# Flash-style attention on one core: exact exponentials of VectorE's low parts in PSUM, side jobs moved, maxima and their rows re-timed

## The chip, the cores and the metric

One core of a Trainium2 chip runs the whole program. The metric is the device time of one execution in microseconds. The kernel before takes 243.28 us, the median of 3 runs (242.67 to 243.59). Engines are named TensorE (PE), VectorE (DVE), ScalarE (ACT), GpSimd (POOL) and SyncE (SP, which issues the DMAs).

## The reference

For each of 8 images `x` of 128 channels and 32 x 32 = 1024 pixels:

```
q = Wq x + bq        (64 x 1024)
k = Wk x + bk        (64 x 1024)
v = Wv x + bv        (128 x 1024)
attn = softmax(q^T k, over the keys)
out  = gamma * (v attn^T) + x
```

All in float32. The kernel keeps the precision by splitting operands into a part rounded to fp32r (hi) and a remainder (lo).

## The kernel before, in words

**Tiling.** An image is 16 steps, 8 images make 128 steps. A step `s` is two key tiles (256 keys) against 256 queries. Four steps (`PART_STEPS`) make a part `u`: the same 256 queries against all 1024 keys; `j` is the place in the part, `k` the place in the image, and a half image (512 queries) is a chunk `c`.

**Stages of a step.** In `score_tile` TensorE computes the scores, transposed, into one of two banks of `scores`: four matmuls of 256 columns (L592 and L593), where the second of each pair adds the low part of q and, in one extra row, minus the maximum. ScalarE's `exponentials` reads them twice: it writes the exact exponential `weight` (L778) and the rounded one `weight_hi` (L781), in a ring of 8 steps. A subtraction makes `weight_lo` in bf16, on GpSimd (L472) or, for the steps that `low_on_dve` names, on VectorE (L878). `sums_hi` adds up `weight_hi` times the values (four matmuls of 258 columns, L612), and after the fourth step of a part `sums_lo` adds the low parts (16 matmuls of 130 columns, L626). A part uses two of the four banks of `sums`, and parts take turns. ScalarE copies the columns of the low values out (L787), VectorE inverts, adds (L889, L883) and writes the outputs (`finish`, L903), two steps after the low sums.

**Order of the work.** Every engine has its own queue, written out by hand as a loop over steps. TensorE's loop step `s` issues the scores of step `s + 2` (`AHEAD`), then the maxima of `max_jobs(s)`, then the sums of step `s - 2` (`LAG`), the low sums where `(s - 2) % 4 == 3`, then `side_jobs(s)`. So a step with low sums is one with `s % 4 == 1`. ScalarE's loop step does the exponentials of `s + 2`, the copy of low sums, and its half of the side jobs; VectorE's does its half of the side jobs of `s - 1`, the maxima of `s`, its subtraction for `s + 1`, and the ends of parts; GpSimd's the subtraction for `s + 1` and then one of its own jobs (low part of x, the bias on x turned, values in bf16).

**Maxima.** The exact maximum over the keys of each query is needed before the scores of its chunk: a matmul of 512 columns into a bank of `work` (L548) and a maximum by VectorE (L847), 8 for a chunk, one for each query tile and half of the keys. They run about a chunk and a half ahead, mostly one to a step; `EARLY_MAXES` is the table for steps 0 to 17. For image 0 TensorE turns the column of maxima into a row ("mt" jobs, L553), which ScalarE writes into `q_lomax`; later ones go by DMA (`send_max_row`).

**The two work banks.** Maxima and side jobs share two banks, taken in the strict turn of `WORK_ORDER`. Each job waits in `take_bank` until the job two places before it has been read out: for a maximum by VectorE's maximum, for "qk" (projection of q and k, L535 to L537) by VectorE's `qk_lo` (L838), which itself follows ScalarE's rounding (L743), for "v" (L542) by VectorE's `v_lo` (L843), which follows L754.

**DMAs.** SP issues everything from one queue in program order: `spread(n)` copies the rounded q and k of image n to their places on other partitions after the last qk job of n and after all scores of image n-2; its first four DMAs (L341 to L345) release the first maxima of image n, the other two its scores.

## Time and profile before

| what | value |
|---|---|
| median of 3 runs | 243.28 us (242.67 to 243.59) |
| the profiled execution: its time | 242.75 us |
| its span on the core | 241.0 us |
| TensorE busy, matmuls | 224.3 us, 93% |
| VectorE busy | 182.1 us, 76% |
| ScalarE busy | 176.9 us, 73% |
| GpSimd busy | 190.3 us, 79% |
| L878, VectorE's low parts | 30 times, 47.7 us, mean 1590 ns |
| L472, GpSimd's low parts | 98 times, 133.9 us, mean 1388 ns |
| chain that ended last | TensorE 74%, VectorE 15%, no visible wait 5%, ScalarE 3% |

How to read it: the span is what the profiler saw on the core, the execution's own time is 1.75 us longer. Matmul rows show how long one takes from start to end; in a dense stretch the next one starts long before, so the distance between starts tells the throughput. A row of the timeline gives the start in us, the duration, engine, line, operation, output and inputs, and in brackets the idle time before it and what ended it. The scores group that begins TensorE's loop step `s` marks the beginning of that step: step 6 begins at 27.50, step 16 at 54.58, step 32 at 82.85, step 38 at 91.88, step 45 at 103.83, step 46 at 107.71, step 48 at 110.18 and step 57 at 123.52.

### The profile page before, as it was taken

To read this page: it belongs to the slowest core of one execution; us is meant where nothing else is said; L and a number is where in the kernel's file an instruction comes from. 1 tells how busy PE (TensorE), PEld (TensorE's weight loads), DVE (VectorE), ACT (ScalarE), POOL (GpSimd) and SP (SyncE) were. 2 spreads that over 40 slices of the span, in tenths; PEclk is the share of its full clock that TensorE was granted. 3 is DMA by queue.
4 is the path that set the end of the run, shared out by engine and by line. 5 is a ranking of instruction groups with operands and counts; after the bars stand their busy time and mean duration, and the time that the engine had idled before them with its cause. 6 is when DMAs were issued, how large, how long until landed. Compare 5 with 4: busy or idle time off the path is not lost.

```text
span 241.0 us, 5343 instructions
## 1 busy us (share of the span) xinstructions
PE 224.3 (93%) x1864; PEld 207.2 (86%) x1864; DVE 182.1 (76%) x341; ACT 176.9 (73%) x342; POOL 190.3 (79%) x165
## 2 busy tenths in 40 slices
PE   6798946999998999989998999989999999999994
PEld 5466936888998999989998999989998999999994
DVE  1678396778888698779888698778898697689224
ACT  2488950675878688768888688768888688778980
POOL 8759991576898689879898689878898677897782
PEclk9999995899999999999999999999999999999999
DMA  3657600058510946048520847039400853010111
GB/s 104 186 222 169 182 0 0 4 119 191 167 51 3 222 85 218 2 99 209 125 98 0 209 98 220 2 86 221 127 10 0 192 116 131 4 44 3 44 48 44
DMA packets 17882, 24.43 MB, mean 101 GB/s; under 512 B 9920, under 2 KB 10688, under 8 KB 17856
## 3 DMA queue, kind: packets, MB, share of 16 engines
q1 hardware_dynamic: 17552, 23.96, 38.3%
q8 instruction: 15, 0.25, 0.4%
q10 hardware_dynamic: 304, 0.13, 0.2%
q14 instruction: 11, 0.09, 0.1%
HBM read 8.59 MB, written 4.19 MB: 53 GB/s over the span
## 4 chain that ended last, share of the span: by engine, by line
PE 74%; DVE 15%; issue 5%; ACT 3%; DMA 1%; ACTq 0%
PE sums L612 21%; PE sums L626 13%; PE work L548 10%; PE scores L592 10%; PE scores L593 9%; DVE neg_max L847 8%; PE work L542 6%; DVE weight_lo L878 4%; ACT values L754 2%; DVE y_sb L903 1%; DMA w_qk<-in_L_conv_Wk 1%; PE sums L548 1%; PE scores L644 1%; PE work L644 1%; PE work L536 0%
## 5 line engine op out<-in xcount | busy, mean ns | idle before, releaser
L472 POOL TENSOR_TENSOR weight_lo<-weight,weight_hi 128x512 bf16<-128x512 f32 x98 | 133.9, 1388 | 14.7 <-ACT weight_hi L781 14.7
L778 ACT ACTIVATE weight<-scores 128x512 f32<-128x512 f32 x128 | 76.9, 601 | 8.4 <-PE scores L593 2.0
L847 DVE TENSOR_REDUCE neg_max<-work 128x1 f32<-128x512 f32 x120 | 80.3, 682 | 3.3 <-PE work L548 3.3
L612 PEld LDWEIGHTS sums<-values,weight_hi 128*128 128x128 f32 x504 | 77.1, 190 | 4.7
L612 PE MATMUL sums<-values,weight_hi 128*128 128x258 f32 x504 | 81.0, 283 | 0.0
L781 ACT ACTIVATE weight_hi<-scores 128x512 fp32r<-128x512 f32 x128 | 77.0, 601 | 0.0
L592 PE MATMUL scores<-q_hihi,k_hilo 128*128 128x256 f32 x256 | 69.6, 294 | 0.0
L593 PE MATMUL scores<-q_lomax,k_hione 128*128 128x256 f32 x256 | 66.2, 281 | 0.0
L548 PE MATMUL work<-k_hilo,q_hihi 128*128 128x512 f32 x120 | 49.4, 416 | 9.9 <-DVE neg_max L847 9.2
L592 PEld LDWEIGHTS scores<-q_hihi,k_hilo 128*128 128x128 f32 x256 | 48.3, 189 | 1.3 <-issue 0.8
L593 PEld LDWEIGHTS scores<-q_lomax,k_hione 128*128 128x128 f32 x256 | 48.5, 189 | 0.8 <-issue 0.2
L878 DVE TENSOR_TENSOR weight_lo<-weight,weight_hi 128x512 bf16<-128x512 f32 x30 | 47.7, 1590 | 0.0
L626 PE MATMUL sums<-values_b,weight_lo 128*128 128x130 bf16 x496 | 35.2, 224 | 0.0
L548 PEld LDWEIGHTS work<-k_hilo,q_hihi 128*128 128x128 f32 x120 | 22.6, 189 | 13.9 <-DVE neg_max L847 7.6
L787 ACT ACTIVATE low_sum<-sums 128x256 f32<-128x256 f32 x31 | 11.9, 385 | 29.3 <-PE sums L626 29.3
L626 PEld LDWEIGHTS sums<-values_b,weight_lo 128*128 128x128 bf16 x496 | 29.7, 99 | 1.5
L889 DVE RECIPROCAL one_over<-sums 128x2 f32<-128x2 f32 x31 | 5.3, 171 | 31.5 <-ACT low_sum L787 31.2
L464 POOL TENSOR_SCALAR values_b<-values 128x512 bf16<-128x512 f32 x16 | 9.9, 620 | 20.4 <-ACT values L754 20.4
L453 POOL TENSOR_TENSOR x_lo<-x_sb,x_hi 128x512 fp32r<-128x512 f32 x12 | 15.5, 1292 | 7.1 <-ACT x_hi L750 7.1
L480 POOL TENSOR_TENSOR x_turned_sb<-x_turned_sb,gamma_bv 128x512 f32<-128x512 f32 x16 | 20.6, 1289 | 0.0
L903 DVE SCALAR_TENSOR_TENSOR y_sb<-sums,one_over,x_turned_sb 128x128 f32<-128x128 f32 x62 | 18.7, 343 | 0.7 <-DVE sums L883 0.4
L843 DVE TENSOR_TENSOR values<-work,values 128x512 fp32r<-128x512 f32 x14 | 9.7, 692 | 10.2 <-ACT values L754 10.2
(82 smaller groups left out, 165.2 us busy)
## 6 DMA issues: line engine op xcount, KB each, us to landing
x_turned_sb<-in_x_turned SPq DMA_DIRECT2D x8, 512.0 KB, 5.5
out<-y_sb SPq DMA_DIRECT2D x15, 256.0 KB, 2.8
x_sb<-in_x SPq DMA_DIRECT2D x7, 512.0 KB, 4.7
q_hihi<-qk_hi SPq DMA_DIRECT2D x12, 256.0 KB, 4.3
q_lomax<-qk_lo SPq DMA_DIRECT2D x7, 256.0 KB, 5.6
k_hione<-qk_hi SPq DMA_DIRECT2D x7, 256.0 KB, 5.4
k_hilo<-qk_hi SPq DMA_DIRECT2D x6, 256.0 KB, 3.2
k_hilo<-qk_lo SPq DMA_DIRECT2D x6, 256.0 KB, 6.2
```

The source lines that it names most:

```text
L472: pool.tensor_tensor(weight_lo[:, r], weight[:, r], weight_hi[:, r], ALU.subtract).then_inc(weight_lo_pool_done, 1)
L480: pool.tensor_tensor(place, place, bias, ALU.add).then_inc(with_bias_done, 1)
L548: pe.matmul(place, q_hihi[p][:, tile(t)], k_hilo[p][:, chunk(h)], start=True, stop=True).then_inc(mx_done, 1)
L592: pe.matmul(place, k_hilo[p][:, keys], q_hihi[p][:, queries], start=True, stop=False)
L593: last = pe.matmul(place, k_hione[p][:, keys], q_lomax[p][:, queries], start=False, stop=True)
L612: last = pe.matmul(sums[:, u % 2 * PAIR + it, 0:VCOLS], weight_hi[:, r, part_tile(kt, it)], values[p][:, key_tile(s, kt)], start=(j == 0 a ...
L626: last = pe.matmul(sums[:, u % 2 * PAIR + it, CHANNELS:VCOLS], weight_lo[:, i % RING, part_tile(kt, it)], values_b[p][:, key_tile(i, kt)], ...
L778: act.activation(weight[:, r], scores[:, s % 2], ACT.Exp)
L781: act.activation(weight_hi[:, r], scores[:, s % 2], ACT.Exp).then_inc(weight_hi_done, 1)
L847: dve.reduce_max(neg_max[:, t, h:h + 1], place, AX.X, negate=True).then_inc(neg_max_done, 1)
L878: dve.tensor_tensor(weight_lo[:, r], weight[:, r], weight_hi[:, r], ALU.subtract).then_inc(weight_lo_done, 1)
L903: dve.scalar_tensor_tensor(y_sb[:, h, at], sums[:, u % 2 * PAIR + it, CHANNELS:2 * CHANNELS], one_over[:, u % 2, it:it + 1], x_turned_sb[: ...
```

## The change

Four things are changed together.

1. `low_on_dve` names every third step of a part (`s % 4 == 2`), from the first part on: 32 steps for 30. For these steps ScalarE writes the exact exponential into the second bank of `sums` that the part is going to use (`exact_weights`), and VectorE subtracts from there. ScalarE waits first until the outputs of the part that used the bank before are written; TensorE waits for the subtraction before the first sums of the part.
2. The side jobs move: qk from steps 8 and 12 of an image to 6 and 10, v from 9 and 13 to 11 and 15. The jobs of ScalarE and GpSimd that feed them or follow them move too.
3. A chunk's maxima alternate between the two halves of the keys (`max_place`), image 0's second chunk is done one a step, the doubled ones lie at steps 7, 8, 11, 12 and 15, and its rows are turned two tiles at a time (`MAX_TURNS`).
4. At the start, image 1's projections of q and k move from ahead of the loop into steps 1 and 2, the second half of image 0's low q is made by one instruction of VectorE out of PSUM, and ScalarE takes the first exponentials ahead of the second q.

```diff
--- before.py
+++ after.py
@@ -37,8 +37,7 @@
 FIRST = ["k0", "q0", "k1", "q1"]
 
 
-DVE_LOW = (0, 4, 8, 12)
-ALL_ON_POOL = 8
+DVE_LOW = 2
 
 
 SPREAD_MX, SPREAD_REST = 4, 2
@@ -46,15 +45,17 @@
 
 
 EARLY = 18
-EARLY_MAXES = {0: (1, 1, 2), 1: (1, 3, 2), 2: (1, 5, 2), 3: (1, 7, 1),
-               6: (2, 0, 1), 7: (2, 1, 2), 8: (2, 3, 1), 9: (2, 4, 1), 10: (2, 5, 1), 11: (2, 6, 2),
-               12: (3, 0, 1), 13: (3, 1, 1), 14: (3, 2, 1), 15: (3, 3, 2), 16: (3, 5, 1), 17: (3, 6, 2)}
+EARLY_MAXES = {0: (1, 1, 1), 1: (1, 2, 1), 2: (1, 3, 1), 3: (1, 4, 1), 4: (1, 5, 1), 5: (1, 6, 1), 6: (1, 7, 1),
+               7: (2, 0, 2), 8: (2, 2, 2), 9: (2, 4, 1), 10: (2, 5, 1), 11: (2, 6, 2),
+               12: (3, 0, 2), 13: (3, 2, 1), 14: (3, 3, 1), 15: (3, 4, 2), 16: (3, 6, 1), 17: (3, 7, 1)}
+
+MAX_TURNS = {0: ("mt", 0, 1), 3: ("mt", 1, 0), 7: ("mt", 1, 1)}
 
 
 def max_jobs(s):
 
     if s < EARLY:
-        c, first, count = EARLY_MAXES.get(s, (0, 0, 0))
+        c, first, count = EARLY_MAXES[s]
         return [(c, i) for i in range(first, first + count)]
     chunk = (s + 14) // TILES
     return [(chunk, (s + 14) % TILES)] if chunk < CHUNKS else []
@@ -64,14 +65,12 @@
 
     b, k = divmod(s, STEPS)
     jobs = []
-    if b == 0 and k == 0:
-        jobs.append(("mt", 0, 1))
-    if b == 0 and k == 4:
-        jobs.append(("mt", 1, 0))
-    if k in (8, 12) and b + 2 < BATCHES:
-        jobs.append(("qk", b + 2, (8, 12).index(k)))
-    if k in (9, 13) and b + 1 < BATCHES:
-        jobs.append(("v", b + 1, (9, 13).index(k)))
+    if s in MAX_TURNS:
+        jobs.append(MAX_TURNS[s])
+    if k in (6, 10) and b + 2 < BATCHES:
+        jobs.append(("qk", b + 2, (6, 10).index(k)))
+    if k in (11, 15) and b + 1 < BATCHES:
+        jobs.append(("v", b + 1, (11, 15).index(k)))
     return jobs
 
 
@@ -91,7 +90,7 @@
 
 
 def low_on_dve(s):
-    return s >= ALL_ON_POOL and s % STEPS in DVE_LOW
+    return s % PART_STEPS == DVE_LOW
 
 
 def low_count(s):
@@ -117,7 +116,11 @@
 
 def max_place(i):
 
-    return i % CHUNK_TILES, i // CHUNK_TILES
+    return i // HALVES, i % HALVES
+
+
+def turn_count(c, half):
+    return HALVES * c + half + 1
 
 
 def half_count(n, h):
...
@@ -277,6 +281,10 @@
 
         def part_banks(u):
             return slice(u % 2 * PAIR, (u % 2 + 1) * PAIR)
+
+        def exact_weights(s):
+
+            return sums[:, s // PART_STEPS % 2 * PAIR + 1]
 
         def key_tile(s, kt):
             return s % PART_STEPS * PAIR + kt
...
@@ -433,13 +441,9 @@
                 pool.wait_ge(pool_setup, made + 4)
                 pool.memset(k_hione[p][HEAD:HEAD + 1, :].bitcast(fp32), 1.0).then_inc(pool_setup, 1)
                 made += 5
-            def first_q_lo(h):
-                pool.wait_ge(first_hi_done, FIRST.index(f"q{h}") + 1)
-                pool.wait_ge(first_q_done, h + 1)
-                pool.tensor_tensor(q_lomax[0][0:HEAD, chunk(h)], q_first[:, h], q_hihi[0][0:HEAD, chunk(h)],
-                                   ALU.subtract).then_inc(first_q_lo_done, 1)
-
-            first_q_lo(0)
+            pool.wait_ge(first_q_done, 1)
+            pool.tensor_tensor(q_lomax[0][0:HEAD, chunk(0)], q_first[:, :], q_hihi[0][0:HEAD, chunk(0)],
+                               ALU.subtract).then_inc(first_q_lo_done, 1)
             pool.wait_ge(pool_setup, made)
             pool.wait_ge(rest_loaded, 3 * 16)
             pool.tensor_scalar(gamma_bv[:, :], b_v[:, :], gamma_col[:, :], 1.0, ALU.mult, ALU.mult).then_inc(pool_setup, 1)
@@ -493,16 +497,14 @@
                     low_weights(s + 1)
                 if s == 0:
                     short_values(0, 1)
-                if s == 1:
-                    first_q_lo(1)
-                if s in (4, 6):
-                    add_bias((4, 6).index(s))
-                if k in (11, 15) and b + 1 < BATCHES:
-                    add_bias(2 * (b + 1) + (11, 15).index(k))
-                if k in (3, 7) and b + 2 < BATCHES:
-                    rest_of_x(b + 2, (3, 7).index(k))
-                if k in (10, 14) and b + 1 < BATCHES:
-                    short_values(b + 1, (10, 14).index(k))
+                if k in (0, 12) and s > 0 and b + k // 12 < BATCHES:
+                    short_values(b + k // 12, 1 - k // 12)
+                if s in (4, 8):
+                    add_bias((4, 8).index(s))
+                if b == 0 and k in (5, 9) or b > 0 and k in (1, 5) and b + 2 < BATCHES:
+                    rest_of_x(b + 2, (5, 9).index(k) if b == 0 else (1, 5).index(k))
+                if b == 0 and k in (10, 13) or b > 0 and k in (9, 13) and b + 1 < BATCHES:
+                    add_bias(2 * (b + 1) + k // 13)
 
         @block.tensor
         def _(pe):
...
@@ -606,6 +608,7 @@
                 if j == 0:
 
                     wait(pe, y_done, PAIR * (u - 1))
+                    pe.wait_ge(weight_lo_done, low_count(s + DVE_LOW))
                 pe.wait_ge(weight_hi_done, s + 1)
                 for kt in range(PAIR):
                     for it in range(PAIR):
@@ -684,9 +687,6 @@
             pe.wait_ge(first_hi_done, len(FIRST))
             for name, c, i in FIRST_MAXES:
                 do_max(c, i)
-            for h in range(HALVES):
-                pe.wait_ge(neg_max_done, CHUNK_TILES + PAIR + h + 1)
-                project_qk(1, h, sums[:, PAIR + h])
 
             for s in range(ALL_STEPS + LAG):
                 if s + AHEAD < ALL_STEPS:
@@ -705,6 +705,9 @@
                     sums_hi(s - LAG)
                     if (s - LAG) % PART_STEPS == PART_STEPS - 1:
                         sums_lo(s - LAG)
+                if s in (1, 2):
+                    pe.wait_ge(neg_max_done, CHUNK_TILES + PAIR + s)
+                    project_qk(1, s - 1, sums[:, PAIR + s - 1])
                 if s < ALL_STEPS:
                     for job in side_jobs(s):
                         do_job(job)
@@ -765,17 +768,21 @@
                 elif name == "v":
                     round_v(n, i, bank(bank_of(job)))
                 elif name == "mt":
-                    if n == 0:
-                        write_max_rows(2, 0, PART, CHUNK, bank(bank_of(job)))
-                    else:
-                        write_max_rows(3, CHUNK, 0, CHUNK, bank(bank_of(job)))
+                    write_max_rows(turn_count(n, i), n * CHUNK, i * PART, (i + 1) * PART, bank(bank_of(job)))
 
             def exponentials(s):
                 r = s % RING
                 act.wait_ge(scores_done, s + 1)
                 if s >= RING:
                     wait_low(act, s - RING)
-                act.activation(weight[:, r], scores[:, s % 2], ACT.Exp)
+                if low_on_dve(s):
+                    u = s // PART_STEPS
+                    wait(act, y_done, PAIR * (u - 1))
+                    if u == 0:
+                        act.wait_ge(neg_max_done, CHUNK_TILES + PAIR)
+                    if u == 1:
+                        act.wait_ge(qk_lo_done, HALVES)
+                act.activation(exact_weights(s) if low_on_dve(s) else weight[:, r], scores[:, s % 2], ACT.Exp)
 
                 wait(act, hi_step, s - RING + 1)
                 act.activation(weight_hi[:, r], scores[:, s % 2], ACT.Exp).then_inc(weight_hi_done, 1)
@@ -795,13 +802,10 @@
                 act.wait_ge(first_done, FIRST.index(f"q{h}") + 1)
                 act.activation(q_hihi[0][:, chunk(h)], place, ACT.Identity, bias=b_qq[:, :]).then_inc(first_hi_done, 1)
 
-            def first_whole_q(h, place):
-                act.activation(q_first[:, h], place[0:HEAD, :], ACT.Identity, bias=b_qq[0:HEAD, :]).then_inc(first_q_done, 1)
-
             first_k(0)
             first_q(0, bank(1))
-            first_whole_q(0, bank(1))
             first_k(1)
+            act.activation(q_first[:, :], bank(1)[0:HEAD, :], ACT.Identity, bias=b_qq[0:HEAD, :]).then_inc(first_q_done, 1)
             act.wait_ge(w_turned, 2)
             act.activation(w_v_t[:, :], bank(0)[:, 0:128], ACT.Copy, scale=gamma_col[:, :]).then_inc(w_v_ready, 1)
             round_v(0, 0, scores[:, 0])
@@ -809,25 +813,23 @@
 
             act.wait_ge(pool_setup, SETUP_MADE)
             write_max_rows(1, 0, 0, PART, scores[:, 1])
+            exponentials(0)
             first_q(1, bank(0))
-            exponentials(0)
             round_v(0, 1, sums[:, 0])
             exponentials(1)
-            round_qk(1, 0, sums[:, PAIR])
-            first_whole_q(1, bank(0))
 
             for s in range(ALL_STEPS):
                 b, k = divmod(s, STEPS)
                 if s + AHEAD < ALL_STEPS:
                     exponentials(s + AHEAD)
-                if s == 0:
-                    round_qk(1, 1, sums[:, PAIR + 1])
+                if s in (1, 2):
+                    round_qk(1, s - 1, sums[:, PAIR + s - 1])
                 if s >= LAG and (s - LAG) % PART_STEPS == PART_STEPS - 1:
                     take_low_sum((s - LAG) // PART_STEPS)
                 for job in side_jobs(s):
                     do_job(job)
-                if k in (2, 6) and b + 2 < BATCHES:
-                    round_x(b + 2, (2, 6).index(k))
+                if b == 0 and k in (4, 8) or b > 0 and k in (0, 4) and b + 2 < BATCHES:
+                    round_x(b + 2, (4, 8).index(k) if b == 0 else (0, 4).index(k))
 
             store_last(act, 1)
 
@@ -846,12 +848,17 @@
             def maximum(t, h, place):
                 dve.reduce_max(neg_max[:, t, h:h + 1], place, AX.X, negate=True).then_inc(neg_max_done, 1)
 
+            def round_second(half):
+                cols = slice(CHUNK_TILES + half * PAIR, CHUNK_TILES + (half + 1) * PAIR)
+                dve.wait_ge(neg_max_done, MAXES + CHUNK_TILES * (half + 1))
+                dve.tensor_reduce(neg_max_r[:, cols], neg_max[:, cols], AX.X, ALU.min).then_inc(neg_max_r_done, 1)
+
             def round_max(c):
                 cols = quarter(c % HALVES)
                 dve.wait_ge(neg_max_done, MAXES * (c + 1))
 
                 if c < 2 * HALVES:
-                    wait(dve, mt_done, c if c >= HALVES else 0)
+                    dve.wait_ge(mt_done, HALVES * (c - 1))
                 else:
                     wait_max_row(dve, c - HALVES)
                 dve.tensor_reduce(neg_max_r[:, cols], neg_max[:, cols], AX.X, ALU.min).then_inc(neg_max_r_done, 1)
@@ -861,7 +868,9 @@
                 dve.wait_ge(mx_done, max_count(c, i))
                 tile_of, keys = max_place(i)
                 maximum(h * CHUNK_TILES + tile_of, keys, bank(bank_of(("mx", c, i))))
-                if i == MAXES - 1:
+                if c == 1 and i % CHUNK_TILES == CHUNK_TILES - 1:
+                    round_second(i // CHUNK_TILES)
+                if c > 1 and i == MAXES - 1:
                     round_max(c)
 
             def do_job(job):
@@ -875,7 +884,7 @@
                 r = s % RING
                 dve.wait_ge(weight_hi_done, s + 1)
                 wait_lo_summed(dve, s - RING)
-                dve.tensor_tensor(weight_lo[:, r], weight[:, r], weight_hi[:, r], ALU.subtract).then_inc(weight_lo_done, 1)
+                dve.tensor_tensor(weight_lo[:, r], exact_weights(s), weight_hi[:, r], ALU.subtract).then_inc(weight_lo_done, 1)
 
             def add_low(u):
                 dve.wait_ge(low_sum_done, u + 1)
@@ -940,12 +949,14 @@
             for n in range(CHUNK_TILES, MAXES):
                 first_maximum(n)
             first_round_max(1)
-            for name, c, i in FIRST_MAXES:
-                do_max(c, i)
+            dve.wait_ge(first_hi_done, len(FIRST))
+            dve.scalar_tensor_tensor(q_lomax[0][0:HEAD, chunk(1)], bank(0)[0:HEAD, :], b_qq[0:HEAD, :],
+                                     q_hihi[0][0:HEAD, chunk(1)], ALU.add, ALU.subtract).then_inc(first_q_rest_done, 1)
             dve.wait_ge(v_hi_done, HALVES)
             dve.tensor_tensor(values[0][:, quarter(1), 0:CHANNELS], by_tiles(sums[:, 0]),
                               values[0][:, quarter(1), CHANNELS:2 * CHANNELS], ALU.subtract).then_inc(first_v_rest_done, 1)
-            rest_of_qk(1, 0, sums[:, PAIR])
+            for name, c, i in FIRST_MAXES:
+                do_max(c, i)
 
             for s in range(ALL_STEPS):
                 b, k = divmod(s, STEPS)
@@ -954,8 +965,8 @@
                         do_job(job)
                 for c, i in max_jobs(s):
                     do_max(c, i)
-                if s == 0:
-                    rest_of_qk(1, 1, sums[:, PAIR + 1])
+                if s in (1, 2):
+                    rest_of_qk(1, s - 1, sums[:, PAIR + s - 1])
                 if s + 1 < ALL_STEPS and low_on_dve(s + 1):
                     low_weights(s + 1)
                 if s >= LAG and (s - LAG) % PART_STEPS == PART_STEPS - 1:
```

## Rows read from the trace of the kernel before

**Rows 1.** The page, part 1: engine, busy us, share of the span, instructions.

```profile
PE 224.3 (93%) x1864; PEld 207.2 (86%) x1864; DVE 182.1 (76%) x341; ACT 176.9 (73%) x342; POOL 190.3 (79%) x165
```

**Rows 2.** List of waits: us in total, times, longest.

```profile
PE work L548 <- DVE neg_max L847: 9.2, 7, 5.6
```

**Rows 3.** Timeline of VectorE, steps 8, 43 and 115: start, duration.

```profile
30.91 6.64 DVE L878 TENSOR_TENSOR weight_lo<-weight,weight_hi 128x512 bf16<-128x512 f32 x1
...
102.70 1.72 DVE L878 TENSOR_TENSOR weight_lo<-weight,weight_hi 128x512 bf16<-128x512 f32 x1
...
222.00 0.69 DVE L878 TENSOR_TENSOR weight_lo<-weight,weight_hi 128x512 bf16<-128x512 f32 x1
```

**Rows 4.** Windows: length, busy of PE, PEld, DVE, ACT, POOL, granted clock, DMA.

```profile
32.00:36.00 4.00, 0.73 (x6) 0.48 (x4) 4.00 (x1) 1.66 (x3) 4.00 (x5) 1.00 0.00 0
36.00:40.00 4.00, 1.70 (x8) 1.54 (x9) 3.92 (x6) 0.00 (x0) 1.00 (x1) 0.58 0.00 0
```

**Rows 5.** Timeline of TensorE in image 0.

```profile
22.73 0.65 PE L612 MATMUL sums<-values,weight_hi 128*128 128x258 f32 x4
...
27.50 0.37 PE L592 MATMUL scores<-q_hihi,k_hilo 128*128 128x256 f32 x1
...
38.30 0.77 PE L548 MATMUL work<-k_hilo,q_hihi 128*128 128x512 f32 x1 [5.57 <-DVE neg_max L847]
...
43.15 0.50 PE L592 MATMUL scores<-q_hihi,k_hilo 128*128 128x256 f32 x1
```

**Rows 6.** Timeline of TensorE in the images behind it.

```profile
54.58 0.28 PE L592 MATMUL scores<-q_hihi,k_hilo 128*128 128x256 f32 x1
...
82.85 0.28 PE L592 MATMUL scores<-q_hihi,k_hilo 128*128 128x256 f32 x1
...
91.88 0.37 PE L592 MATMUL scores<-q_hihi,k_hilo 128*128 128x256 f32 x1
...
98.60 1.11 PE L542 MATMUL work<-w_v_t,x_sb 128*128 128x128 f32 x8
...
103.83 0.28 PE L592 MATMUL scores<-q_hihi,k_hilo 128*128 128x256 f32 x1
...
105.08 0.50 PE L548 MATMUL work<-k_hilo,q_hihi 128*128 128x512 f32 x1 [0.62 <-DVE neg_max L847]
...
107.71 0.36 PE L592 MATMUL scores<-q_hihi,k_hilo 128*128 128x256 f32 x1
...
110.18 0.28 PE L592 MATMUL scores<-q_hihi,k_hilo 128*128 128x256 f32 x1
...
110.66 0.39 PE L548 MATMUL work<-k_hilo,q_hihi 128*128 128x512 f32 x1
...
114.03 0.39 PE L548 MATMUL work<-k_hilo,q_hihi 128*128 128x512 f32 x1
...
123.52 0.28 PE L592 MATMUL scores<-q_hihi,k_hilo 128*128 128x256 f32 x1
...
124.14 0.50 PE L548 MATMUL work<-k_hilo,q_hihi 128*128 128x512 f32 x1
```

**Rows 7.** Durations: VectorE's L843 alone (min/median/max), two groups of ScalarE.

```profile
L843 DVE TENSOR_TENSOR values<-work,values x14: 691/692/694, 44.2 to 215.3; 128x512 fp32r<-128x512 f32 x14
...
L778 ACT ACTIVATE weight<-scores 128x512 f32<-128x512 f32 x128 | 76.9, 601 | 8.4 <-PE scores L593 2.0
...
L750 ACT ACTIVATE x_hi<-x_sb 128x512 fp32r<-128x512 f32 x12 | 7.6, 633 | 0.0
```

**Rows 8.** Timeline of VectorE: the low parts of v and of qk.

```profile
100.38 0.69 DVE L843 TENSOR_TENSOR values<-work,values 128x512 fp32r<-128x512 f32 x1 [0.67 <-ACT values L754]
...
124.44 0.75 DVE L838 SCALAR_TENSOR_TENSOR qk_lo<-work,b_qk,qk_hi 128x512 fp32r<-128x512 f32 x1 [0.36 <-ACT qk_hi L743]
```

**Rows 9.** The spread's fourth DMA: one issue, and the landing of all six.

```profile
106.60 1.14 SPq L345 DMA_DIRECT2D k_hilo<-qk_lo  x1
...
DMA to landing us min/median/max: 5.0/6.2/6.8
```

21 lines of the change are left out of this document (11 added, 10 removed).

## The prediction

> **What bounds the kernel now.** I read the page first: TensorE is busy for 224.3 of 241.0 us [rows 1], so only some 17 us, lead-in and tail included, can come from its pauses. In the list of waits the one large entry of TensorE is the matmul of the maxima (L548) waiting for VectorE to read a work bank: 9.2 us in 7 waits, 5.6 of them in one [rows 2]. VectorE's rows explain that one: the subtraction of the low parts in step 8 (L878), two SBUF inputs, lasts 6.64 us at 30.91 where the same instruction takes 0.69 in image 7 and 1.72 in a middle image [rows 3]. In the windows of those microseconds GpSimd is busy for all of 32 to 36 and for the first microsecond behind it, then idle; VectorE is busy with that one instruction, TensorE for 0.73 of 4 us [rows 4]. VectorE got its turn only when GpSimd ran dry. TensorE stood for 5.57 us and came back slow: from the max matmul of step 9 to the next step it took 4.85 us (38.30 to 43.15) [rows 5], against 2.63 for the same work in step 45 (105.08 to 107.71) [rows 6], and the granted clock of 36 to 40 was 0.58 [rows 4], mostly the 1.2 GHz level of the two. So image 0 lost about 5.6 + 2.2 us at one place.
>
> In a middle image TensorE is dense. An image takes 27.33 us (82.85 to 110.18). The max matmul follows the start of its step by 0.48 (110.18 to 110.66), but by 1.25 in step 45 (103.83 to 105.08) and by 0.62 in step 57 (123.52 to 124.14) [rows 6]. So 0.77 + 0.14 = 0.9 us an image is waiting behind the slow subtraction and the side job, and the rest is work. In image 7 nothing of this is left.
>
> **The change, part by part.**
>
> *Exact exponentials in PSUM.* ScalarE writes one 128x512 tile in four to a bank of sums, VectorE subtracts from there. The nearest row is L843, a subtraction with one PSUM and one SBUF input: 691 to 694 ns in all 14, whatever GpSimd did [rows 7]. From below the uncontested 0.69 with two SBUF inputs [rows 3] bounds it, from above the 1.72; I take 0.69. That is 32 x 0.69 = 22 us of VectorE for 30 subtractions of which the middle images' took 1.5 to 1.7. It is not TensorE's time by itself; what counts is that no subtraction stands in front of a maximum for over 0.69 us. GpSimd has 96 of them for 98, and nobody to wait for at the port. ScalarE's write to PSUM: no row has one of its own. It reads PSUM and writes SBUF in 601 ns and goes from SBUF to SBUF in 633 [rows 7], so I take 601, with 30 ns less or more: 1 us in all on an engine idle for a quarter of the span, at no cost to the end.
>
> A rule speaks against this edit. The Trainium skill (VectorE: DVE Perf Modes, section on the TRN2 errata) gives a vector instruction with a PSUM source 120 fixed cycles against 58 for SBUF, an estimated 65 ns more, 2 us of VectorE in all. The rows of 0.692 and 0.69 [rows 3, 7] show no such difference, and the sum is the same by either, since that engine would hide it. On the port, the same notes (SBUF — State Buffer, on the two sides of SBUF) say that GpSimd and a two-SBUF-input vector instruction exclude each other for one whole instruction; the 6.64 us show that the loser can lose several rounds, which is the case that costs here.
>
> *New waits.* ScalarE's exponential of step 4u+2 waits for the outputs of part u-2, and everything behind it in its queue with it. Their last instruction lands about 2.35 us after the start of step 4u-2 on TensorE (low sum, two small ops, one maximum, two output ops), the scores it needs land at 3.05: margin 0.7. TensorE's first sums of part u wait for that subtraction. It ends about 3.5 us after the start of step 4u and is wanted at 4.1: margin 0.6. I cost both at nothing in the steady part; what hides them is that TensorE's own step with low sums is long.
>
> *Side jobs.* qk goes to 6 and 10, v to 11 and 15. The second v now takes the bank of the qk job one step before. In the trace qk's low part is written at 125.19 (124.44 + 0.75), 1.67 us after the step that follows qk began (123.52) [rows 6, 8]. A plain step is 1.19, so v waits 0.5 in step 11. After v, its low part lands 2.47 us after v began (98.60 to 101.07) [rows 6, 8], just in time for the second max behind it. So a middle image loses 0.9 us of waits and gains 0.5: **0.4 us, four images, 1.6 us**. Image 1 also has a doubled max in its second step now, which becomes single: it took 28.27 us (54.58 to 82.85) against 27.33, so 0.9 more, **1.4 us** with its 0.4 rounded up. Image 6 has only v jobs and no such wait, image 7 none: nothing, though GpSimd's last three subtractions become two, up to 0.2 at the end.
>
> *Start.* Image 1's qk projections leave the place ahead of step 0, and image 0's second q loses one ScalarE and one GpSimd op for one op of VectorE. Followed by the durations above: scores 3 land at 19.0 and their exponentials end at 20.1, the rounding of qk (0.69) at 20.7, its low part (0.75) at 21.5, and only then comes the subtraction of step 2, 22.15. The first sums start there (before: 22.73 [rows 5]), after 1.6 us of idle. Behind them stand the second projection (0.66), two maxima turns and one read-out wait (0.3): step 6 starts at 28.5, 1.0 us later than before (27.50 [rows 5]). From step 6 to 16 the same jobs took 18.3 us in image 2 (91.88 to 110.18 [rows 6]), 17.4 without waits. To that come five second maxima at 0.24 (1.2), a turned row (0.15), and second maxima waiting for the low parts of qk in steps 7 and 11 (1.67 - 0.71, 1.0 each) and of v in step 12 (0.85). Step 16 starts at 50.1 instead of 54.58 [rows 6]: **4.5 us**.
>
> *DMAs.* No transfer is added, but SP's spread of the next image waits for step 13's scores, and the maxima of k=2 for its fourth DMA. Before, that DMA was issued 2.8 us after step 45 began (106.60) and landed 5.0 to 6.8 later [rows 9], with the max due 10.2 after that beginning (114.03 [rows 6]). Now due at 9.4, issued some 0.2 earlier, so landing at 7.6 to 9.4: just hidden, at no cost.
>
> **Sum.** 4.5 + 1.4 + 1.6 + 0.2 = 7.7 us of the profiled execution's 242.75, so 235.05. The median of the runs shown is 0.5 above that execution, so I say 235.5. The measurement tells about 0.5%, 1.2 us, from nothing.
>
> **The rivals.**
> *The clock falls at the start* (chance 0.14). The new 1.6 us pause around 21 us, with another near 1 us before step 1, might cost TensorE its 2.4 GHz. For it: a clock of 0.58 after the hole. Against it: that hole was 5.6 us. Price as above 2.2 us: 237.7.
> *The spread is late* (0.13). Margins of 0 to 1.8 us; half a microsecond late in six images is 3 us: 238.5. Against it: only the slowest landing reaches the due time.
> *v does not wait behind qk* (0.12). If ScalarE and VectorE are both quicker there, five images keep 0.5: 233.0. Against it: 1.67 us is a chain of matmul, rounding and subtraction with almost no slack in it.
> *The change doesn't free VectorE* (0.04). If a subtraction with one SBUF input is held off as well, the hole stays somewhere: about 243. Against it: 692 ns, 14 times.
> *Slower* (0.05). ScalarE's wait for the outputs of part u-2 becomes the bound: it then holds back the next exponentials, they hold back the scores. Each microsecond over the 0.7 margin costs all 31 parts; from 0.25 us a part it eats the gain. A waiting v remainder in front of the outputs (1.37 us, 0.67 over) would give 31 x 0.67 = 21 less 7.7, some 256 us. Against it: that remainder stands in steps 0 and 12, not where the outputs are made.
>
> **How the numbers follow.** My forecast has 0.52. The first three rivals bring it to 0.91, from 233.0 to 238.5. The start is the least certain term (1 us either way), and it makes the tails; with 0.3 and 0.2 us for the spread of runs beyond the two outer cases I give 232.7 to 238.7, and expect two in ten outside. Faster by over 0.5% is all but the last two cases: 0.91, within 0.5% 0.04, slower 0.05.
>
> **What would show it.** Right: L878 at 0.69 us with hardly any spread; no idle time of TensorE over 2 us behind the lead-in and a granted clock of 1.0 at 36 to 44 us; step 16 near 50 us; a wait of 0.5 us ahead of v (L542) for VectorE's qk_lo in step 11, none ahead of L548 in step 13; L472 shorter than its 1.39. Wrong: subtractions over 1 us, waits of L778 on VectorE's y_sb, of L612 on weight_lo outside the start, or of L548 on a DMA.

## The result and the profile after

The changed kernel takes 240.0 us (median of 17 runs, 239.2 to 242.66) against 242.75 us for the kernel before in the same comparison (17 runs, 242.1 to 243.71). The ratio is 0.9896, with a 95% interval of 0.9873 to 0.9919. So the change is a gain of 1.0%, or 2.5 us (the medians differ by 2.75). I forecast 235.5 us and a range of 232.7 to 238.7: the direction was right, the size was three times too large, and the range missed.

The page of the changed kernel, parts 1, 2 and 5 (the columns are those of rows 1; in part 5 count, busy us, mean ns, then the idle time before the group and what ended it):

```profile
span 238.0 us, 5352 instructions
...
PE 221.8 (93%) x1864; PEld 205.0 (86%) x1864; DVE 161.0 (68%) x345; ACT 177.9 (75%) x342; POOL 177.5 (75%) x162
...
PEclk9999999999999999999999999999999999999999
...
L476 POOL TENSOR_TENSOR weight_lo<-weight,weight_hi 128x512 bf16<-128x512 f32 x96 | 123.1, 1290 | 40.7 <-ACT weight_hi L788 40.6
...
L887 DVE TENSOR_TENSOR weight_lo<-sums,weight_hi 128x512 bf16<-128x512 f32 x32 | 22.0, 686 | 6.6 <-ACT weight_hi L788 6.6
```

VectorE's subtraction (L878 before, L887 now) has fallen from a mean of 1590 ns to 686, GpSimd's (L472 before, L476 now) from 1388 to 1290. The two engines lost 21 and 13 us of busy time, and the granted clock is 0.9 or more in every slice, where [rows 4] had 0.58. All of that is as intended, and yet only 3.0 us of the span are gone.

The clock is not as steady in every execution. In twelve of the 17 the mean granted clock is 0.998 or more, and they take 239.2 to 240.4 us. In the other five it is 0.990 to 0.993, and they take 239.6 to 242.7, with a median of 241.5.

Where the gain went shows in the starts of TensorE's steps (L592 before, L594 now), read from the timelines of both and from those of the experiments in the same way:

| stretch, us | before | changed | forecast |
|---|---|---|---|
| up to step 0 | 17.23 | 16.48 | |
| step 0 to 6 | 10.27 | 12.61 | |
| step 0 to 16 (image 0) | 37.35 | 37.43 | |
| start of step 16 | 54.58 | 53.91 | 50.1 |
| image 1 | 28.27 | 26.99 | 26.9 |
| image 2 | 27.33 | 27.03 | 26.9 |
| image 6 | 24.81 | 24.82 | 24.8 |

The start of step 0 is read from one execution each and scatters: it lies between 16.1 and 17.4 us in the nine traces with the new start (mean 16.6), and between 16.8 and 18.4 in the five with the old one (mean 17.5).

Images 1 to 6 came out as forecast, within 0.15 us each. Image 0 lost its hole of 5.6 us and the slow clock behind it, and took as long as before. The timeline of ScalarE and TensorE in image 0 of the changed kernel names what took its place:

```profile
32.72 0.69 ACT L746 ACTIVATE qk_hi<-work,b_qk 128x512 fp32r<-128x512 f32 x1 [1.78 <-DMA k_hione<-qk_hi]
...
38.14 0.58 ACT L785 ACTIVATE sums<-scores 128x512 f32<-128x512 f32 x1 [2.33 <-DVE y_sb L912]
```

```profile
22.44 0.72 PE L615 MATMUL sums<-values,weight_hi 128*128 128x258 f32 x4 [1.66 <-DVE weight_lo L887]
...
29.09 0.37 PE L594 MATMUL scores<-q_hihi,k_hilo 128*128 128x256 f32 x1
...
34.34 0.47 PE L550 MATMUL work<-k_hilo,q_hihi 128*128 128x512 f32 x1 [2.41 <-DVE qk_lo L840]
...
41.36 0.47 PE L537 MATMUL work<-x_hi,w_qk_hi 128*128 128x512 f32 x1 [0.46 <-POOL x_lo L457]
...
43.87 0.50 PE L550 MATMUL work<-k_hilo,q_hihi 128*128 128x512 f32 x1 [0.87 <-DVE qk_lo L840]
...
47.16 0.50 PE L550 MATMUL work<-k_hilo,q_hihi 128*128 128x512 f32 x1 [0.71 <-DVE values L845]
...
53.91 0.36 PE L594 MATMUL scores<-q_hihi,k_hilo 128*128 128x256 f32 x1
```

Two of these waits are not in the forecast. ScalarE rounds image 2's first qk job in step 6 into the staging buffer `qk_hi`, and has to wait until image 1's spread has been read out of it (the two waits in `round_qk` for the first half of an image): 1.78 us. And its exponential of step 10 waits 2.33 us for the outputs of part 0. The pauses for the subtraction of step 2 (1.66), for qk's low part in step 11 (0.87) and for v's in step 12 (0.71) are the forecast ones, and so is a part of the 2.41 in step 7. The 0.46 in step 10 follows from the wait for the outputs: it is gone in `e1_finish0`.

### The profile page after: what moved, and what is told of

The parts are those of the page before. It is cut to its first block, busy times and chain, and to the rows that moved or that the text cites. A ratio compares the mean times of both kernels' runs of the same rounds, so it can differ in the third digit from the quotient of the medians.

```text
span 238.0 us, 5352 instructions
## 1 busy us (share of the span) xinstructions
PE 221.8 (93%) x1864; PEld 205.0 (86%) x1864; DVE 161.0 (68%) x345; ACT 177.9 (75%) x342; POOL 177.5 (75%) x162
## 4 chain that ended last, share of the span: by engine, by line
PE 80%; DVE 6%; ACT 4%; DMA 3%; issue 3%; POOL 2%; SPq 1%; ACTq 0%; POOLq 0%
PE sums L615 22%; PE sums L629 12%; PE scores L594 11%; PE scores L595 11%; PE work L550 10%; PE work L544 6%; ACT qk_hi L746 2%; DVE qk_lo L840 2%; DMA k_hione<-qk_hi 2%; DMA w_qk<-in_L_conv_Wk 1%; PE work L537 1%; PE work L539 1%; PE work L538 1%; PE sums L550 1%; DVE neg_max L849 1%
## 5 line engine op out<-in xcount | busy, mean ns | idle before, releaser
L476 POOL TENSOR_TENSOR weight_lo<-weight,weight_hi 128x512 bf16<-128x512 f32 x96 | 123.1, 1290 | 40.7 <-ACT weight_hi L788 40.6
L849 DVE TENSOR_REDUCE neg_max<-work 128x1 f32<-128x512 f32 x120 | 82.0, 686 | 12.2 <-PE work L550 12.2
L594 PE MATMUL scores<-q_hihi,k_hilo 128*128 128x256 f32 x256 | 71.0, 300 | 0.5 <-ACT weight_hi L788 0.5
L785 ACT ACTIVATE weight<-scores 128x512 f32<-128x512 f32 x96 | 57.5, 599 | 10.0 <-PE scores L595 3.6
L550 PE MATMUL work<-k_hilo,q_hihi 128*128 128x512 f32 x120 | 48.4, 406 | 4.7 <-DVE qk_lo L840 3.3
L594 PEld LDWEIGHTS scores<-q_hihi,k_hilo 128*128 128x128 f32 x256 | 48.3, 189 | 2.1 <-issue 1.6
L629 PE MATMUL sums<-values_b,weight_lo 128*128 128x130 bf16 x496 | 34.4, 221 | 0.0
L629 PEld LDWEIGHTS sums<-values_b,weight_lo 128*128 128x128 bf16 x496 | 28.9, 98 | 1.4
L887 DVE TENSOR_TENSOR weight_lo<-sums,weight_hi 128x512 bf16<-128x512 f32 x32 | 22.0, 686 | 6.6 <-ACT weight_hi L788 6.6
L785 ACT ACTIVATE sums<-scores 128x512 f32<-128x512 f32 x32 | 19.0, 592 | 3.0 <-DVE y_sb L912 2.3
L544 PE MATMUL work<-w_v_t,x_sb 128*128 128x128 f32 x112 | 15.4, 280 | 2.0 <-DVE qk_lo L840 1.9
```

The source lines that it names most:

```text
L476: pool.tensor_tensor(weight_lo[:, r], weight[:, r], weight_hi[:, r], ALU.subtract).then_inc(weight_lo_pool_done, 1)
L544: last = pe.matmul(place[:, tile(t)], image(n)[:, tile(half * CHUNK_TILES + t)], w_v_t[:, :], start=True, stop=True)
L550: pe.matmul(place, q_hihi[p][:, tile(t)], k_hilo[p][:, chunk(h)], start=True, stop=True).then_inc(mx_done, 1)
L594: pe.matmul(place, k_hilo[p][:, keys], q_hihi[p][:, queries], start=True, stop=False)
L629: last = pe.matmul(sums[:, u % 2 * PAIR + it, CHANNELS:VCOLS], weight_lo[:, i % RING, part_tile(kt, it)], values_b[p][:, key_tile(i, kt)], ...
L785: act.activation(exact_weights(s) if low_on_dve(s) else weight[:, r], scores[:, s % 2], ACT.Exp)
```

## The experiments

Each kernel ran beside the kernel before on the same chip; ratios are to that kernel. Line numbers shift by up to eleven between the kernels.

**Outputs of part 0 two steps earlier** (`e1_finish0`), in the changed kernel:

```diff
-    return PART_STEPS * part + PART_STEPS + AHEAD + (2 if part == 0 else 0)
+    return PART_STEPS * part + PART_STEPS + AHEAD
```

> The changed kernel with the outputs of part 0 at step 6 instead of step 8. Theory (the change put a new wait on ScalarE: the exponential of step 10 waits 2.33 us for the outputs of part 0, which stand two steps later than those of any other part): that wait falls to nothing, the low part of x and the second qk job come earlier, steps 9 and 10 shrink from 2.74 and 2.66 us towards 2.1 and 2.0, and the time falls by 1.0 to 1.5 us against the changed kernel's 240.0, to about 238.8. Rival (all of image 0's loss comes from the landing of image 1's spread, and this wait only stands in its shadow): within 0.3 us of the changed kernel.

Ratio 0.9819 (0.9790 to 0.9849), 239.07 us against 243.09; the changed kernel's ratio is 0.9896. That is 0.8%, or 1.9 us, under the changed kernel by the ratios, and image 0 is 1.6 us shorter. The exponential of step 10 follows its scores after 0.16 us, steps 9 and 10 take 2.10 and 1.97 us, and image 0 takes 35.81. The theory holds, with a gain a little above the expected one. The other wait stays where it was: rounding in step 6 starts after 1.49 us of idle, and TensorE waits 2.12 us for it.

**Image 0's qk jobs at steps 8 and 12** (`e2_qk8`), in the changed kernel:

```diff
-    if k in (6, 10) and b + 2 < BATCHES:
-        jobs.append(("qk", b + 2, (6, 10).index(k)))
+    qk_at = (8, 12) if b == 0 else (6, 10)
+    if k in qk_at and b + 2 < BATCHES:
+        jobs.append(("qk", b + 2, qk_at.index(k)))
```

> The changed kernel with image 0's two qk jobs back at steps 8 and 12. Theory (rounding qk of image 2 in step 6 waits 1.78 us until image 1's spread has landed at 32.65 us, because the staging buffer qk_hi is still being read): the wait goes to under 0.3 us, step 7 shrinks from 4.18 us to about 2.5, and the time falls by 1.0 to 1.6 us to about 238.7; the wait for part 0's outputs stays. Rival (the second maxima of the doubled steps set the pace anyway): no change within 0.4 us.

Ratio 0.9746 (0.9721 to 0.9771), 237.16 us. That is 1.5% under the changed kernel, twice what I expected: image 0 takes 34.83 us for 37.43. Step 7 is down to 1.78 us from 4.18, and step 8 is up to 2.56 from 1.50, since qk now stands there. The edit does more than the theory asks for: it also takes away TensorE's waits for qk's low part in steps 7 and 11, 1.0 each in the forecast, so it does not price the wait for the spread alone.

**Both edits** (`e3_both`).

> The changed kernel with both edits: outputs of part 0 at step 6, image 0's qk jobs at steps 8 and 12. Theory (the two waits are what kept image 0 3.8 us behind the forecast, and they add): step 16 starts near 51.2 us instead of 53.9, time 237.0 to 237.6. Rival (they overlap, one hides the other): 238.5 to 239.

Ratio 0.9731 (0.9701 to 0.9761), 236.73 us, 0.3 us below what was expected. Image 0 takes 33.82 us, 3.6 less than in the changed kernel. Laid behind the changed kernel's start of step 0, that puts step 16 at 50.3 us. That this is near the forecast of 50.1 is partly luck, because the pauses behind qk, which the forecast has, are gone here as well. The two edits don't quite add. In the time of the whole run 0.8% and 1.5% give 1.65%, with intervals of 0.3% either way, and in image 0 1.6 and 2.6 us give 3.6.

**The exact exponentials back in SBUF** (`e4_sbuf`), every wait and job where the change has it:

```diff
-            return sums[:, s // PART_STEPS % 2 * PAIR + 1]
+            return weight[:, s % RING]
```

> The changed kernel with the exact exponentials of VectorE's steps back in the SBUF ring, every wait and every job where it is. Theory (port contention with GpSimd is what the PSUM bank buys): VectorE's subtraction goes from 0.69 us mean to 1.4 to 1.8 with some above 2.5, GpSimd's from 1.29 back to about 1.37, and because TensorE's first sums of a part now wait for it with a margin of 0.6 us, most parts lose some tenths: 243 to 248 us. Rival (what mattered was one unlucky run of GpSimd work at step 8, the other subtractions are hidden): under 0.8 us slower than the changed kernel.

Ratio 1.0046 (1.0025 to 1.0067), 244.36 us: 1.5% above the changed kernel, and above the kernel before. VectorE's subtractions as the trace lists them (min/median/max ns), in this run and in the changed kernel:

```profile
L887 DVE TENSOR_TENSOR weight_lo<-weight,weight_hi x32: 680/769/1601, 21.1 to 234.2; 128x512 bf16<-128x512 f32 x32
```

```profile
L887 DVE TENSOR_TENSOR weight_lo<-sums,weight_hi x32: 679/690/693, 21.5 to 230.8; 128x512 bf16<-128x512 f32 x32
```

The time is in the expected range, but the subtraction is not as long as I said: 994 ns on average instead of 1.4 to 1.8 us, none above 1.6. GpSimd's went back to 1400 ns. Middle images take 27.70 us for 27.03, and all of it is in two steps: the third of the image takes 1.69 us for 1.28, the seventh 2.24 for 1.97. In these two parts the subtraction lasts 1.27 and 1.47 us, and TensorE's first sums of the part come right behind its end. The rows of the first of them:

```profile
84.52 1.27 DVE L887 TENSOR_TENSOR weight_lo<-weight,weight_hi 128x512 bf16<-128x512 f32 x1
```

```profile
86.02 0.54 PEld L615 LDWEIGHTS sums<-values,weight_hi 128*128 128x128 f32 x4 [0.48 <-issue]
```

So the PSUM bank is worth 1.5% even in a placement where no subtraction is held for long. The other half of this reading matters as much: both inputs are in SBUF here, and the hole of 5.6 us does not come back. In this order of the work it does not take PSUM to be rid of it.

**The first v job at step 12** (`e5_both_v12`), on top of both edits:

```diff
-    if k in (11, 15) and b + 1 < BATCHES:
-        jobs.append(("v", b + 1, (11, 15).index(k)))
+    if k in (12, 15) and b + 1 < BATCHES:
+        jobs.append(("v", b + 1, (12, 15).index(k)))
```

> The run with both edits (outputs of part 0 at step 6, image 0's qk jobs at 8 and 12), and besides the first v job of every image at step 12 instead of 11, so that it no longer takes the work bank of the qk job right before it. Theory (v in step 11 waits about 0.6 us for qk's low part; the steady images lose that once each): step 11 of a middle image shrinks from 2.64 us, an image from 27.0 to 26.5 us, 5 images: about 2.5 us less than the run with both edits, 234.2. Rival (the wait only moves: the maximum of step 12 or 14 then waits for qk's or v's low part): under 0.7 us less, and a new wait of L550 on VectorE.

Ratio 0.9609 (0.9586 to 0.9633), 233.64 us. Step 11 falls from 2.64 us to 1.18 (v is gone from it), and an image from 27.0 to 26.5. In image 2 of this run, first the maximum of step 12 waits a little (its start is 0.55 behind step 12's, for 0.48 in a plain step), then v runs freely:

```profile
96.53 0.50 PE L551 MATMUL work<-k_hilo,q_hihi 128*128 128x512 f32 x1
97.34 1.05 PE L545 MATMUL work<-w_v_t,x_sb 128*128 128x128 f32 x8
```

Against the run with both edits that is 1.2%, or 3.0 us, for the 2.5 expected. Theory upheld in size. But 26.5 is not the floor, as the next run shows.

**The PSUM part of the change alone, in the kernel before** (`e6_before_psum`). This is item 1 of the change as a whole: the source moves to PSUM, and VectorE's subtractions move with it, from the first to the third step of a part.

```diff
-DVE_LOW = (0, 4, 8, 12)
-ALL_ON_POOL = 8
+DVE_LOW = 2
...
+                    pe.wait_ge(weight_lo_done, low_count(s + DVE_LOW))
...
-                act.activation(weight[:, r], scores[:, s % 2], ACT.Exp)
+                if low_on_dve(s):
+                    u = s // PART_STEPS
+                    wait(act, y_done, PAIR * (u - 1))
...
+                act.activation(exact_weights(s) if low_on_dve(s) else weight[:, r], scores[:, s % 2], ACT.Exp)
```

> The kernel before with one part of the change: VectorE takes every step with s % 4 == 2, exact exponentials in the bank of sums, with the waits that go with it; side jobs, maxima, start as before. Theory (the PSUM source frees VectorE from the port): VectorE's subtractions at 0.69 us, the hole of 5.6 us and the fall of the clock behind it are gone, step 45 shorter; ScalarE waits for the outputs of part 0 in step 8 as in the changed kernel. 8 us for the hole less 1 to 2 for that wait, plus up to 0.7 us in 5 images: 234 to 237 us against 243.1. Rival (the placement of side jobs was as much part of the cure): 239 to 241 us.

Ratio 0.9483 (0.9455 to 0.9510), 230.47 us against 243.01: 5.2% under the kernel before, and 3.5 us under the low end that I gave. That end was added up wrongly: 7 us for the hole and the wait and 3.5 for the images, off 243.1, give 232.6. Image 0 takes 30.48 us for 37.35, which is the 7. The five images give 6.1 us instead of 3.5: 1.1 in each of four, which now take 26.2, and 1.7 in image 1. This is the run that tells what happened to the change: its first item alone is worth 12.5 us, and the rest of it gives 10 back. What the run does not tell is which half of the item does it, the PSUM source or the new steps of VectorE. A maximum in step 45 stood behind a subtraction of 1.72 us before, and has none in front of it now. No run has two SBUF inputs, the new steps and the old side jobs together. VectorE's row of the page, and the timeline of TensorE in step 45 up to the start of step 46:

```profile
L889 DVE TENSOR_TENSOR weight_lo<-sums,weight_hi 128x512 bf16<-128x512 f32 x32 | 21.9, 686 | 7.7 <-ACT weight_hi L792 7.7
```

```profile
95.78 0.28 PE L595 MATMUL scores<-q_hihi,k_hilo 128*128 128x256 f32 x1
...
96.25 0.39 PE L551 MATMUL work<-k_hilo,q_hihi 128*128 128x512 f32 x1
...
97.93 1.11 PE L545 MATMUL work<-w_v_t,x_sb 128*128 128x128 f32 x8
98.79 0.36 PE L595 MATMUL scores<-q_hihi,k_hilo 128*128 128x256 f32 x1
```

With the old places the max matmul of step 45 follows its step by 0.47 us, where [rows 6] had 1.25: the trace shows no wait in the step at all, which takes 3.01 us instead of 3.88. v stands one step behind qk there too, but that step also holds the low sums, so v comes 2.15 us after the step's start and finds its bank read (wanted: 1.67, as in [rows 8] against the 123.52 of [rows 6]). The same v in the changed kernel, in a step without low sums (step 43, which starts at 98.62):

```profile
100.35 1.16 PE L544 MATMUL work<-w_v_t,x_sb 128*128 128x128 f32 x8 [0.39 <-DVE qk_lo L840]
```

**Step 8's subtraction given to GpSimd** (`e7_pool12`), in the kernel before:

```diff
-ALL_ON_POOL = 8
+ALL_ON_POOL = 12
```

> The kernel before with one number changed: VectorE's subtractions begin at step 12 instead of step 8, so step 8's is GpSimd's. No PSUM, no other move. Theory (the one subtraction of step 8 starved by five GpSimd instructions in a row cost about 8 us): GpSimd's queue is 1.3 us longer there, VectorE doesn't starve, TensorE's hole of 5.6 us goes to under 1.5 us and the clock stays: 235.5 to 238 us. Rival (GpSimd is the bottleneck at that place, and TensorE would wait for its low parts instead; or step 12's subtraction starves likewise): 240 to 243 us.

Ratio 0.9950 (0.9924 to 0.9976), 241.89 us: the rival. Step 9 now takes 3.00 us for 11.06, and the hole has moved to the next subtraction of VectorE, in step 12. VectorE's row, GpSimd's rows from the same microseconds and TensorE's wait:

```profile
38.91 5.32 DVE L878 TENSOR_TENSOR weight_lo<-weight,weight_hi 128x512 bf16<-128x512 f32 x1
```

```profile
38.69 1.33 POOL L480 TENSOR_TENSOR x_turned_sb<-x_turned_sb,gamma_bv 128x512 f32<-128x512 f32 x1
39.93 3.75 POOL L472 TENSOR_TENSOR weight_lo<-weight,weight_hi 128x512 bf16<-128x512 f32 x3
```

```profile
44.89 0.79 PE L548 MATMUL work<-k_hilo,q_hihi 128*128 128x512 f32 x1 [4.42 <-DVE neg_max L847]
```

It ends when GpSimd has run dry, as in [rows 3, 4]. So the hole is not tied to step 8. In both places where it was seen, VectorE's first subtraction with two SBUF inputs met four or five GpSimd instructions in an unbroken row.

**The subtraction of step 2 ahead of qk's low part** (`e9_both_lowfirst`), on top of both edits:

```diff
+                if s + 1 < ALL_STEPS and low_on_dve(s + 1):
+                    low_weights(s + 1)
                 if s in (1, 2):
                     rest_of_qk(1, s - 1, sums[:, PAIR + s - 1])
-                if s + 1 < ALL_STEPS and low_on_dve(s + 1):
-                    low_weights(s + 1)
```

> The run with both edits, and besides VectorE does the subtraction of step 2 ahead of the low part of image 1's first qk job. Theory (TensorE's first sums wait 1.66 us for that subtraction only because it stands behind an op that waits for ScalarE): L615 starts near 20.6 us instead of 22.4, of which 1.0 to 1.7 us reach the end: 235.1 to 235.8. Rival (the second projection of image 1 and ScalarE's exponentials 4 and 5 bound the start): under 0.5 us less.

Ratio 0.9670 (0.9647 to 0.9692), 235.06 us. The first sums start at 20.94, steps 0 to 6 take 10.99 us for 12.62, and all 1.6 us of it reach step 16. Theory upheld: the pause was a matter of order in one queue.

**The PSUM part with the early outputs** (`e8_before_psum_fin`): the kernel of `e6_before_psum` with the edit of `e1_finish0`.

> The kernel before with the PSUM part of the change alone, and the outputs of part 0 at step 6 instead of step 8. Theory (ScalarE's exponential of step 10 waits 1.58 us for those outputs, after which qk's low part and with it the v job of step 9 are late): step 9 shrinks from 3.76 us towards 3.0, 0.6 to 1.0 us less than the same kernel with the late outputs, 229.4 to 229.9. Rival (the wait is hidden behind the spread or the max rows): within 0.3 us of 230.5.

Ratio 0.9429 (0.9395 to 0.9462), 229.17 us, the lowest ratio of all, though its interval touches those of `e6_before_psum` and `e12_oldside_fin_low`: 5.7% under the kernel before and 4.7% under the changed one. Image 0 takes 29.77 us for 30.48.

**The changed kernel with the old side jobs** (`e10_after_oldside`), and the rounding of x, its low part, bias and short values with them:

```diff
-    if k in (6, 10) and b + 2 < BATCHES:
-        jobs.append(("qk", b + 2, (6, 10).index(k)))
-    if k in (11, 15) and b + 1 < BATCHES:
-        jobs.append(("v", b + 1, (11, 15).index(k)))
+    if k in (8, 12) and b + 2 < BATCHES:
+        jobs.append(("qk", b + 2, (8, 12).index(k)))
+    if k in (9, 13) and b + 1 < BATCHES:
+        jobs.append(("v", b + 1, (9, 13).index(k)))
```

> The changed kernel with its side jobs, and the jobs that feed them, back in their old places (qk 8 and 12, v 9 and 13), everything else as changed. Theory (moving the side jobs is a loss once the port is free: v behind qk waits 0.6 us and qk behind plain steps 0.2 us in every image with both, and in image 0 the rounding of qk waits for the spread): middle images at 26.25 us instead of 27.0, step 7 under 2.6 us, in all 5 to 6 us less than the changed kernel: 234 to 235. Rival (the old places were good only with the old start): above 237.

Ratio 0.9562 (0.9520 to 0.9605), 232.58 us, 1.4 us below the expected range. Middle images take 26.2 us, as expected, and image 0 takes 33.76, 3.7 less than in the changed kernel.

**The PSUM part with the new side jobs, old start** (`e11_before_psum_newside`): the kernel of `e6_before_psum` with the reverse of that diff.

> The complement: the kernel before with the PSUM part and the side jobs moved as in the change, start and maxima as before. Theory: middle images at 27.0 us, 3.5 to 4 us lost in five images against 230.5; in image 0 the spread of image 1 is issued 2.8 us earlier than in the changed kernel, so the rounding of qk waits less than 1.8 us there; 234 to 236. The rest up to the changed kernel's 240 is then the price of the new start and the new order of maxima. Rival (the new places cost only together with the new start): 231 to 232.5.

Ratio 0.9723 (0.9686 to 0.9761), 236.61 us, 0.6 above the expected range. Middle images take 27.0 us, image 0 32.63. ScalarE's rounding in step 6 does not wait for the spread here, only for its matmul: the last transfer of image 1's spread is issued at 23.24 us, in the changed kernel at 27.84. TensorE's wait in step 7 is 0.86 us for 2.41. The wait for the outputs of part 0 is there, 2.90 us:

```profile
30.02 0.69 ACT L747 ACTIVATE qk_hi<-work,b_qk 128x512 fp32r<-128x512 f32 x1 [0.30 <-PE work L540]
...
34.57 0.58 ACT L789 ACTIVATE sums<-scores 128x512 f32<-128x512 f32 x1 [2.90 <-DVE y_sb L914]
```

**The changed kernel with every found wait taken out** (`e12_oldside_fin_low`): old side jobs, early outputs, the subtraction of step 2 first.

> The changed kernel with the old places of the side jobs, the outputs of part 0 at step 6, and VectorE's subtraction of step 2 ahead of qk's low part: every wait that I have found, taken out, with the new start kept. Theory (what is left of the new start is about neutral): 231.5 to 233.5. If the new start is a gain by itself: under 230. Rival (the new start and the single maxima cost by themselves): above 234.

Ratio 0.9453 (0.9412 to 0.9493), 229.93 us. Image 0 takes 31.43 us, 1.7 more than the 29.77 of `e8_before_psum_fin`. Image 1 gives 0.5 of that back (26.15 for 26.61), and the earlier step 0 some 0.9 by the means above. By the letter of the expectation, 229.93 is just "under 230" and the new start a gain by itself. But the old start with the early outputs is at 229.17, and the two can't be told apart by these intervals: cleaned of its waits, the new start is neutral.

Together the four kernels that have PSUM and differ in side jobs and start (with the order of the maxima) are a square:

| ratio to before | old side jobs | new side jobs |
|---|---|---|
| old start | 0.9483 | 0.9723 |
| new start | 0.9562 | 0.9896 (the change) |

## Why the prediction was wrong, point by point

**What bounds the kernel: right.** The 6.64 us subtraction stood there because GpSimd went first, and `e7_pool12` shows the same in a second place. With one PSUM input the subtraction takes 0.69 us in all 32 places and in both schedules, and no slow stretch of the clock is left in the profiled execution. That PSUM is what ended the hole is not shown: `e4_sbuf` has no hole either.

**The cost of the subtraction: right.** 0.69 us was forecast, 686 ns measured, 679 to 693. By the Trainium skill (VectorE: DVE Perf Modes, section on the TRN2 errata) it would be an estimated 65 ns longer than the SBUF form. The two are level to 1 ns at their minimum, 679 here and 680 in `e4_sbuf`, so the measurement decides against it here.

**ScalarE's write to PSUM: right in size.** 593 ns median against 599 to SBUF, by the 32 and 96 instructions of L785 in the changed kernel.

**Steady images: right as a sum.** I took 0.4 us an image and 1.4 for image 1; measured were 0.3 and 1.3. The wait of v behind qk, put at 0.5, is 0.6: step 11 takes 2.64 us for the 1.99 of step 47, where v does not wait. The maximum two steps after qk, which my sum does not have, adds 0.18 in step 8.

**Start and image 0: the step that failed.** I gave it 4.5 us; measured between step 0 and step 16 it is nothing, and 0.7 with the earlier step 0. Of the 3.8 us between my 50.1 and the measured 53.91, 0.6 are the start itself (step 6 at 29.09, not 28.5). The other 3.2 are in steps 6 to 16, which took 24.82 us for the 21.6 of my sum, and the two waits that I left out account for them. The wait for part 0's outputs is worth 1.6 us of image 0 by `e1_finish0`. The wait for the spread is worth about 1.6: TensorE's pause in step 7 is 2.41 us with it and 0.86 in `e11_before_psum_newside` without it. With `e3_both`, which takes out both waits and the pauses behind qk too, the stretch takes 21.20. Both showed in signs that the prediction had named: a wait of ScalarE on VectorE's y_sb, and an idle time of TensorE over 2 us.
- Under *DMAs* I asked who waits for the spread to land, and looked at its readers alone, the maxima. Its source has a waiter too. `round_qk` may overwrite the staging buffer only after the transfers have read it. The change moved image 1's projections later and image 2's first qk job earlier, so the two met. Neither move does it alone: `e11_before_psum_newside` rounds in step 6 without that wait, and `e10_after_oldside`, with the new start, rounds in step 8, and its list of waits has none.
- Under *New waits* I worked out a margin of 0.7 us for the outputs of part u-2 and wrote that I cost it at nothing "in the steady part". I never worked it out for part 0, whose outputs `finish_step` puts two steps later than all others. There the margin was negative, and the wait 2.33 us.

**The comparison itself: incomplete.** The forecast added up the change against the old waits, part by part, and never asked what the old places of the side jobs would do once item 1 was in. So it gave the gain to the wrong part. I charged the 0.9 us that a middle image lost to "the slow subtraction and the side job" and took them off in the account of the moved side jobs. With item 1 alone, that is with short subtractions in their new steps and no side job moved, TensorE's trace shows no wait over 0.1 us from image 1 to image 6: 26.2 us a middle image, 1.1 less than before and 0.8 less than in the changed kernel. By the square, moving the side jobs costs 2.4% with the old start and 3.3% with the new one, the new start and maxima 0.8 and 1.7%, and the excess of one over the other, 0.9%, is where the spread wait belongs. With four intervals of 0.2 to 0.4% each, that last figure is rough; in the traces image 0 has 1.5 us of it, which fits the wait.

**The rivals.** None of them explains the miss. The clock did not fall in the profiled execution, and twelve of 17 executions have 0.998 or more. In the other five it was lower, and they took 1.7 us more in the median; no trace of them shows where. The spread was not late for the maxima, v did wait, and the subtraction did come free. The rival "slower" had the right mechanism, ScalarE held by the outputs of part u-2, but placed it in every part; it happened in one.

**What stays open.** How much of the first item is the PSUM source and how much the new steps of VectorE, in the old order of the side jobs: the run that would tell is `e6_before_psum` with the exact exponentials in SBUF. Inside the pair "new start and new order of maxima" I did not separate the two: `e12_oldside_fin_low` shows only that, without the waits, they are neutral together. The fastest kernel, `e8_before_psum_fin`, still has TensorE wait 0.44 us in image 0 for a row of maxima that comes by DMA, and nothing was tried on that.

## What to carry to other kernels

Before costing a move, cost the fix alone: if one instruction's length caused the waits, ask what the old order does once it is short, because re-placing the other jobs may then only add waits. When the fix itself has two halves, here a source and a place, run each by itself. A buffer that a DMA reads has a second waiter, the next writer, and it must be checked whenever the writer moves earlier or the transfer later. Work out a margin also for the first and the last round of a loop, where the code has exceptions of its own.

## What the runs showed of the hardware that I had not expected

A vector subtraction with two SBUF inputs doesn't always lose just one turn to GpSimd. In two places it was held for 6.64 and 5.32 us, behind five and four GpSimd instructions, until that engine had no more to do. Everywhere else in these two kernels and in `e4_sbuf` the longest was 1.73 us. By the Trainium skill (SBUF — State Buffer, on the two sides of SBUF) the loser is blocked for the whole instruction of the other. The 1.73 us fit that, one GpSimd instruction of 1.3 and the subtraction's own 0.69 being 2.0 at most; the 6.64 and 5.32 don't, and here the measurement decides. What sets the two places apart is not settled. In both, the first GpSimd subtraction that went ahead had had its input ready for 2.5 and 2.0 us before it began. In the others the next GpSimd subtraction had had it for 0.8 us at most, and where it overlapped the subtraction it took 1.5 to 1.75 us for 1.3. But one of those that went ahead had had its input for only 0.7 us.

The same subtraction with one PSUM input took 678 to 694 ns, 352 times in eleven kernels, whatever GpSimd did.

A longer instruction on an engine that is busy for 68% of the span reached the end for about half. In `e4_sbuf` the first two subtractions of a middle image are together 1.4 us longer than in the changed kernel, and the image is 0.7 us longer, because TensorE waits for them with a small margin. An engine's idle share says little of whether its instructions may grow.
